# Second attention of a fused layer: the router's input rows are split before they are transposed, and a transposing DMA on the SP queue takes the place of TensorE's transposes

## The reference

```
x = x + attention0(layernorm(x), ctx)      # 1 head, biases, softmax over 120 keys
x = x + int8_product(layernorm(x), rhs)    # quantized rows times a quantized 512x512 matrix
x = x + attention1(layernorm(x), ctx)      # 16 heads of 32, softmax over 120 keys, then @ w_o.T
h = layernorm(x)
logits = h @ gate_w.T                      # 9 numbers a row: 8 routed experts and a shared one
x = x + sum of the chosen experts' silu(h Wg) * (h Wu) Wd, weighted by a routing made from the logits
        + the shared expert's (inner width 1024)
```

## Time and profile before

| | |
|---|---|
| median of 3 runs | 1254.04 us (1253.72 to 1260.35) |
| the profiled execution: its own time / its span | 1257.87 us / 1255.9 us |
| TensorE busy, weight load busy | 96% of the span, 67% |
| VectorE, ScalarE, GpSimd busy | 76%, 56%, 46% |
| chain that ended last | TensorE 83%, VectorE 7%, issue 3%, DMA 2%, ScalarE 2% |
| mean granted TensorE clock | 0.991 |

### The profile page before, as it was taken

The page is one execution under the profiler, slowest core; times in us unless marked ns, Lnnn a source line. Parts: engine busy times, 40 slices in busy tenths (PEclk is TensorE's granted clock), DMA queues, the critical chain, the costliest instruction groups (busy, mean ns, idle before and its releaser), DMA issues.

```text
span 1255.9 us, 29496 instructions
## 1 busy us (share of the span) xinstructions
PE 1200.5 (96%) x10772; PEld 836.1 (67%) x10788; DVE 952.0 (76%) x2006; ACT 709.4 (56%) x1988; POOL 583.5 (46%) x685
## 2 busy tenths in 40 slices
PE   6888998889999999999999999999999999999996
PEld 3555664678888888886444444777777777666663
DVE  5889898799999999897677777777777775645451
ACT  4377778699999998896354232222222231555553
POOL 0047677637777777732300000777775200355624
PEclk9999999899999999999999999999999999999999
DMA  9522033133544444543890051222223610688946
GB/s 347 211 68 69 1 33 45 43 94 124 172 148 165 171 157 158 169 157 115 173 206 1 22 147 34 69 35 68 52 52 79 209 68 1 219 174 209 185 54 84
DMA packets 132223, 144.00 MB, mean 115 GB/s; under 512 B 53200, under 2 KB 86128, under 8 KB 132080
## 3 DMA queue, kind: packets, MB, share of 16 engines
q1 hardware_dynamic: 114240, 119.65, 32.2%
q0 software_dynamic: 13248, 21.15, 9.4%
q10 hardware_dynamic: 4592, 1.32, 0.5%
HBM read 84.93 MB, written 57.19 MB: 113 GB/s over the span
## 4 chain that ended last, share of the span: by engine, by line
PE 83%; DVE 7%; issue 3%; DMA 2%; ACT 2%; POOL 1%; SPq 0%; ACTq 0%; DVEq 0%; POOLq 0%
PE bank L121 29%; PE bank L2130 15%; PE bank L2123 13%; PE bank L1503 6%; PE bank L955 4%; PE bank L1435 3%; PE bank L1456 3%; PE bank L1450 2%; PE bank L1421 2%; PE bank L1024 2%; DMA q_rows<-att_land 1%; PE bank L2409 1%; PE bank L872 1%; ACT att_land L1353 1%; PE bank L961 1%
## 5 line engine op out<-in xcount | busy, mean ns | idle before, releaser
L1628 POOL DMA_INDIRECT lists<-att_land x128 | 133.2, 1041 | 208.2 <-DVE att_land L1768 166.8
L1353 ACT ACTIVATE att_land<-bank,att_land 128x120 f32<-128x120 f32 x512 | 178.3, 375 | 13.1 <-DVE att_land L1221 12.9
L2123 PE MATMUL bank<-att_land 128*128 128x512 f16 x768 | 176.2, 379 | 0.6 <-DVE program_logits L1304 0.6
L1950 ACT ACTIVATE att_land<-program_x 128x512 f32<-128x512 f32 x40 | 25.2, 631 | 195.2 <-DVE program_x L2092 195.2
L2123 PEld LDWEIGHTS bank<-att_land 128*128 128x128 f16 x768 | 75.1, 98 | 82.0 <-issue 0.6
L121 PE MATMUL bank<-program_xs,program_wgu 128*128 128x512 f16 x576 | 128.7, 379 | 0.6 <-DVE att_land L1727 0.6
L1353 ACT ACTIVATION_READ_ACCUMULATOR att_land<-bank,att_land 128x1 f32 x512 | 113.1, 222 | 0.0
L1789 POOL DMA_INDIRECT att_land<-xn_rows,att_land x40 | 39.8, 996 | 141.2 <-DMA out_rows<-att_land 96.1
L121 PE MATMUL bank<-att_land 128*128 128x128 f16 (+1 forms) x1560 | 102.8, 223 | 0.5 <-DVE att_land L1278 0.5
L121 PEld LDWEIGHTS bank<-program_xs,program_wgu 128*128 128x128 f16 x576 | 56.2, 98 | 67.5 <-DVE att_land L1727 1.1
L1221 DVE TENSOR_REDUCE att_land<-bank 128x4 f32<-128x480 f32 x128 | 82.2, 643 | 21.7 <-PE bank L1421 21.3
(11 more groups left out here) (303 smaller groups left out, 2857.3 us busy)
## 6 DMA issues: line engine op xcount, KB each, us to landing
att_land<-q_rows SPq DMA_DIRECT2D x96, 128.0 KB, 2.6
xn_rows<-att_land SPq DMA_DIRECT2D x37, 256.0 KB, 3.4
out_rows<-att_land SPq DMA_DIRECT2D x37, 256.0 KB, 6.7
q_rows<-att_land SPq DMA_DIRECT2D x32, 256.0 KB, 2.7
xt_tiles<-att_land SPq DMA_DIRECT2D x32, 256.0 KB, 2.1
x_rows<-program_x SPq DMA_DIRECT2D x8, 1024.0 KB, 5.0
att_land<-x_rows SPq DMA_DIRECT2D x8, 1024.0 KB, 6.9
program_xs<-xt_tiles SPq DMA_DIRECT2D x28, 256.0 KB, 6.0
```

The costliest lines, as they stand in the source:

```text
L1353: last = act.activation(prob[:, c, h, :], ps_s[c % 2][:, h, :], ACT.Exp, bias=nmax[:, u % 2, c, h:h + 1], accum_out=rsum[:, u % 2, n:n + 1])
L1628: pool.indirect_dma_start(out=io["lists"], out_offset=bass.IndirectOffsetOnAxis(ap=index[:, t, k:k + 1], axis=0), in_=load[:, t, k, :], in ...
L2123: last = pe.matmul(ps_y[i][:, :], hid[:, c % 2, a, i * P:(i + 1) * P], wd[:, q, c, :], start=c == 0 and n == 0, stop=c == NC - 1 and n == 2)
```

## The change

The rows are split before they are transposed. ScalarE's `gate_high` copies lg.xn to f16, VectorE's `gate_low` subtracts, both from SBUF into one new buffer `gates` [128, 2, 512] f16. SyncE then issues one transposing DMA, 256 KB from `gates` to gT (one buffer in place of two), and counts it in g_turned. TensorE's `gate_transposed` is gone. `gate_logits(t-5)` moves from the first third of the step to the place where `gate_transposed` stood, and waits for g_turned; its result now lies in bank 6, which it shares with `product`. VectorE's `gate_low` moves from the end of step t (tile t-4) to the front of the step t that follows (tile t-5), ahead of `rows_low`; `logits` moves from the middle of step t (tile t-5) to the front of step t (tile t-6). ScalarE's `gate_high` goes behind `exps(t, 2)`. On SyncE the transposing DMA comes right behind the q_rows store, and the store of xt_tiles waits for it. The stage has one step more at its end (LAG 5 to 6).

```diff
-    gT = g.late(7 * D, [P, 2, 2, KC, P], f16)
+    gT = g.late(7 * D, [P, 2, KC, P], f16)
+    gates = g.late(8 * D, [P, 2, D], f16)
...
-    ps_l = ps_x[:, 0, 0:2 * (E + 1)].rearrange("p (q n) -> p q n", q=2)
+    ps_l = banks[6][:, 0:2 * (E + 1)].rearrange("p (q n) -> p q n", q=2)
...
+            w = t - 5
+            if live(w):
+                sp.wait_ge(s["g_lo"], w + 1)
+                sp.wait_ge(s["g_hi"], w + 1)
+                need(sp, s["l_mm"], w)
+                need(sp, gt_out[(w - 1) % 2], 16 * ((w + 1) // 2))
+                sp.dma_start_transpose(gT[:, :, :, :].rearrange("p q k n -> p (q k) n"),
+                                       gates[:, :, :].rearrange("p q n -> p (q n)")).then_inc(s["g_turned"], 16)
...
-            if live(v):
-                sp.wait_ge(s["g_lo"], v + 1)
-                sp.dma_start(io["xt_tiles"][v, :, :], gT[:, v % 2].rearrange("p q k n -> p (q k n)")).then_inc(gt_out[v % 2], 16)
+            w = t - 5
+            if live(w):
+                sp.wait_ge(s["g_turned"], 16 * (w + 1))
+                sp.dma_start(io["xt_tiles"][w, :, :], gT[:, :, :, :].rearrange("p q k n -> p (q k n)")).then_inc(gt_out[w % 2], 16)
...
-                dve.tensor_tensor(gT[:, u % 2, 1], ps_g[:, :, :], gT[:, u % 2, 0], ALU.subtract).then_inc(s["g_lo"], 1)
+                dve.tensor_tensor(gates[:, 1], lg.xn[:, u % 2], gates[:, 0], ALU.subtract).then_inc(s["g_lo"], 1)
...
             prob_low(t - 1, 0)
+            logits(t - 6)
             query_low(t + 1)
+            gate_low(t - 5)
             rows_low(t + 2)
...
-            logits(t - 5)
...
-            gate_low(t - 4)
...
-                act.wait_ge(s["g_tr"], u + 1)
-                need(act, s["l_mm"], u - 1)
-                need(act, gt_out[u % 2], 16 * (u // 2))
-                act.activation(gT[:, u % 2, 0], ps_g[:, :, :], ACT.Copy).then_inc(s["g_hi"], 1)
+                act.wait_ge(lg.ok, u + 1)
+                need(act, s["g_turned"], 16 * u)
+                act.activation(gates[:, 0], lg.xn[:, u % 2], ACT.Copy).then_inc(s["g_hi"], 1)
...
+            exps(t, 2)
             gate_high(t - 4)
-            exps(t, 2)
...
-        def gate_transposed(u):
-            if live(u):
-                pe.wait_ge(lg.ok, u + 1)
-                need(pe, s["x_new"], min(u + 2, NT))
-                need(pe, s["g_lo"], u)
-                transposed(ps_g, lg.xn[:, u % 2]).then_inc(s["g_tr"], 1)
...
-                pe.wait_ge(s["g_lo"], u + 1)
-                need(pe, s["xt_lo"], min(u + 8, NT))
-                need(pe, s["o_lo"], min(u + 3, NT))
+                pe.wait_ge(s["g_turned"], 16 * (u + 1))
+                need(pe, s["x_new"], min(u + 3, NT))
...
-            gate_logits(t - 5)
...
-            gate_transposed(t - 4)
+            gate_logits(t - 5)
             queries(t + 2, 1)
```

25 lines of the change are left out of this document (12 added, 13 removed).

## The result

The changed kernel takes 1264.44 us (median of 5 runs, 1258.59 to 1266.05) against 1254.04 (1253.67 to 1260.35). The ratio is 1.0057, 95% interval 1.0029 to 1.0085 (it is taken over all runs of both; the two medians alone would give 1.0083). The forecast was 1246.7 us, faster by more than half a per cent. The profiled execution took 1266.05 us, its span is 1264.2, that is 8.3 more than before. In the changed kernel `product` is L1511, `gate_logits` L1523, `rows_low` L1288, `gate_low` L1309, the logits' sum L1314, the transposing transfer L1155, the scores L1430, GpSimd's two operations on the router's rows L1189 and L1192, and the shared expert's first product L2122.

The account below looks back on a forecast made before the run. TensorE, busy 99.6 of 100 us, was taken to set the pace. Terms -12.6 - 0.9 + 4.2 - 0.8 + 2.8 = -7.3 us gave 1246.7 from 1254.04; the 8-in-10 range was 1241 to 1300.

Parts of the forecast that it names:

- transposes off TensorE, per step: First product's steps: the router's transposes leave TensorE, 0.45 us in each of 28 full steps, -12.6 us.
- wait of the queries for `rows_low`: TensorE's queries wait for VectorE, with two operations newly ahead of `rows_low`: 0.15 us a step (0 to 0.30), +4.2 us.
- pitch: Length of a step, between first halves of the product: 10.70 - 0.45 + 0.15 = 10.40 us.
- landing of the transfer: Transposing DMA on SyncE's queue: lands in T = 3.4 us (2.0 to 16), hidden up to 4.86 before TensorE's logits.
- stalls of single steps, t = 6 to 30: Steps held by x stores or key and weight loads ahead of the queries' store: should nearly go, -0.8 us.
- end of the stage: Shared expert's first product waits for the last transposing transfer, itself behind the xt_tiles store with one gT: +2.8 us.
- The main mechanism: First product's steps: transfer lands under 4.86 us and pitch is near 10.40; chance 0.60.
- Rivals 1 and 2: At `gate_logits`: 1, late landing makes TensorE wait each step, 1304 us, 0.27; 2, blocks turned in series, 1571 us, 0.08.
- Rival 3: VectorE's loop: two moved operations cost 0.3 us more a step, GpSimd reading SBUF beside; pitch 10.70, 1255 us, chance 0.05.
- T - 0.6: General form of the end-of-stage cost, T being the transposing transfer's landing time; 2.8 us at T = 3.4.

Follow-up runs that it names:

- e9: Changed kernel with the logits' sum at the end of VectorE's step and both halves of the gate's split back at their old places; 1253.38 us, ratio 0.9978.
- e1: Changed kernel with one call moved: VectorE sums a tile's logits at the end of the step in which TensorE made them; 1260.9 us, ratio 1.0029.
- e10: e9 with token loads one per step, keys and gate/up weights loaded behind the xt_tiles store, x stored one tile a step; 1247.76 us, ratio 0.9929.
- e4: Changed kernel, but from the second tile on only the high halves are transposed by the transfer (128 KB in place of 256 KB); 1259.19 us.
- e11: Changed kernel with only the gate's split back at its old places, the logits' sum left at the front of VectorE's step; 1281.31 us.
- e13: e11 with GpSimd's subtraction on the gate and up weights replaced by a fill with zeros; steps t = 7 to 26 at 10.87 or 10.88 us.
- e3: Changed kernel with ScalarE's four first token loads issued one a step in steps 26 to 29, not all in step 26; 1258.83 us, ratio 1.0012.

## Why the prediction was wrong, step by step

| step of the prediction | predicted | measured |
|---|---|---|
| transposes off TensorE, per step | -0.45 us | -0.44 (e9: 10.26) |
| wait of the queries for `rows_low` | 0.15 | 0.15 (e1); in the changed kernel hidden behind the next |
| wait of the product for the logits' sum | not in the sum | 0.26 a step |
| pitch | 10.40 | 10.52 |
| landing of the transfer | 3.4 (room 4.86) | 3.6, from 3.1 to 6.0 |
| stalls of single steps, t = 6 to 30 | 3.2 - 0.8 = 2.4 us | 9.8 |
| end of the stage | +2.8 | +7.1 (e9, e10: +2.6, +2.7) |

The sum was -7.3 and the two spans differ by +8.3. The misses make that up: 25 steps x 0.12 is 3.0, the stalls 7.4, the end of the stage 4.3, in all 14.7 of 15.6. The pitch alone would have left a gain (-7.3 + 3.0); what turned it into a loss are the stalls and the end.

**The main mechanism was right.** Rivals 1 and 2 are out: 256 KB are turned in 3.6 us, at the price of a plain transfer. By the Trainium skill's 1309 ns for a 128x128 block ("VectorE: DVE Perf Modes", section "The three transpose paths") eight blocks in a row would have made an estimated 10.5 us; the 3.6 measured, and the 3.4 for four blocks (e4), show that they are not done in a row. TensorE's 0.45 us are gained in full once nothing waits (e9).

**The step that failed first**, in the order of the sum, is the pitch: "TensorE waits about 0.15 us in each step". The diff moves the logits to the bank of the product, and I followed the new wait of the transfer and that of `rows_low`, but not `need(pe, s["l_ok"], u - 2)` back through VectorE's order to ScalarE. e1 and e9 show it.

**Rival 3 had the right place and the wrong form.** It named GpSimd reading SBUF beside the split, priced it at 0.3 us a step, and gave it 0.05 because the same operation took 0.69 us with both sources in SBUF. That row is from a stage in which GpSimd mostly did nothing beside it. The block shows on VectorE in 5 of the steps from t = 6 to 30, where the order of two starts 0.1 us apart turns, and costs what is left of the other's instruction: up to 0.8 us in the changed kernel, 1.6 in e11. The Trainium skill has the rule, which I should have weighed there: "SBUF — State Buffer", section "Who interferes with whom", says that a VectorE instruction with two SBUF inputs contends with a GpSimd instruction that reads SBUF, not with one that only writes it, and calls the shared ports an exclusive lock. The traces agree: 0.66 us from PSUM beside the same product, 1.45 and 2.27 from SBUF, and 0.66 beside a fill (e13).

**The stalls** are the largest miss. The prediction said that those by x and the weights "should nearly go". Two of before's did, but one came back as a late transfer (0.98 us), and the largest was not looked at: the four token loads on ScalarE's queue cost 0.81 us of TensorE before and 3.71 now. e3 shows that they are worth 5.7 us. What is not settled is why the same four issues held ScalarE for 3.9 us now. Before, they held it for 2.8. The traffic around them is denser (DMA share 0.96 from 525 to 535, before 0.82); halving the transposing transfer did not shorten the hold (4.33 us in e4), so the cause stays open.

**The end.** The term was worked out for the last transfer alone, at T - 0.6. Four transfers in a row stand there with nothing to cover them; with one gT and one `gates`, each waits for the store before. On top TensorE worked between them at a granted clock of 0.77 to 0.89: the twelve matmuls of L121 took 4.44 and 4.23 us, where such a group took 2.75 before. And the split came a step later: with it back in its place and the same one gT, the end takes 50.6 us (e9, e10). That is +2.7 against before, the size of the term, but by luck: TensorE still waits 2.04, 2.26 and 0.94 us for transfers in e10, and its granted clock falls to 0.87 and 0.96 (590 to 600, 600 to 610). A gain of the size forecast is there in e10 (9.8 us of span; e9 alone has 5.1), but not in the kernel for which it was forecast.

## What to carry to other kernels

When a value changes its buffer, list every new wait for that buffer and follow each back to the engine that is really late: two waits on one path hide one another, so a fix of one alone shows little (0.10) or harm (+0.36), and both together the whole (0.26). When an operand moves from PSUM to SBUF, look at what GpSimd does at that time, and measure the price in a stretch where it works, not in one where it is idle. A transfer that replaces work of a full engine needs room in the queue: look for the bursts that stand ahead of it, and at the end of the loop, where nothing covers it.

## What the runs showed of the hardware

- A transposing transfer of 256 KB (f16, 128 x 1024, SBUF to SBUF) lands in 3.1/3.6/6.0 us (minimum, median, maximum) and holds SyncE's queue for 1.24 us or more (a plain store of the queries for 0.34); half of it lands in 2.5/3.4/5.3.
- VectorE (both sources in SBUF) and GpSimd (reading SBUF) take turns by whole instructions: 0.68 became 1.45 and 2.27, and GpSimd's 1.04 became 1.47 when it came second.
- An engine that issues DMAs can be held by them: two issues took 3.89 us of ScalarE, and 2.77 in the kernel before. One issue a step took 0.53 to 0.59 (e3).
- After waits of 3.7 us (530) and of 2.2 and 2.8 us (607, 615) TensorE's granted clock was at 0.72 and 0.77 over 10 us, between its levels of 1.2 and 2.4 GHz, and matmul groups took 1.6 to 1.9 times as long. These waits cost more than their length.
